# Gate's edge stage: the weighted values of a batch in two PSUM banks instead of SBUF

## The chip, the cores and the metric

The kernel runs on one core of one Trainium2 chip. The metric is the device time of one execution in microseconds; lower is better. The time given is the median of three runs. The profile is of one further execution.

## The reference

The reference is a graph network of four layers over 3125 nodes with 256 features, each a graph step and a mixture of experts. The change lies in the third layer's mixture of experts, whose gate is itself a small graph attention over 65536 edges (numbered below 4096; the nodes are 3125) with 4 heads of 4 values:

```python
h = (x_flat @ W_gat).reshape(M, HEADS, NUM_EXPERTS)      # 4 heads, 4 experts
src = jnp.concatenate([edge_index[0], loops])
dst = jnp.concatenate([edge_index[1], loops])
a_src = (h * att_src).sum(-1)
a_dst = (h * att_dst).sum(-1)
e = jax.nn.leaky_relu(a_src[src] + a_dst[dst], negative_slope=0.2)
e_max = jax.ops.segment_max(e, dst, num_segments=M)
ee = jnp.exp(e - e_max[dst])
denom = jax.ops.segment_sum(ee, dst, num_segments=M)
alpha = ee / (denom[dst] + 1e-16)
msg = h[src] * alpha[:, :, None]
agg = jax.ops.segment_sum(msg, dst, num_segments=M).reshape(M, HEADS * NUM_EXPERTS) + b_gat
```

The scores of the experts come from a layer norm of agg, and the best two of four are taken for each node.

## The kernel before

The program is a chain of phases, each a block in which the five engines (TensorE, VectorE, ScalarE, GpSimd, and SyncE for DMAs) run their own instruction lists and meet at its end. gate_graph calls gate_nodes, gate_edges and gate_scores one after the other. The change is in gate_edges alone.

gate_edges takes the 65536 edges as 512 tiles (GTILES) of 128, one edge on each partition, in 64 batches (NBG) of 8 tiles (GB). A node's row in DRAM, src_rows, has GV = 20 numbers: 16 values (W = 4 heads x 4) and 4 source logits. The destination node is split into a low part (which of 128 partitions) and a high part (which of NT = 25 groups).

The lists are written out by hand; counting semaphores are all that orders one engine behind another. For batch n:

- GpSimd (lines 2601 to 2606) issues 8 indirect DMAs, each of which gathers the 128 source rows of a tile into srow, which holds four batches. Before batch n it waits until batch n-4 has been weighed.
- ScalarE: `turned` (2682) makes hotT, the transposed one-hot of the low part, by Abs and Relu over 1024 columns; `straight` (2691) makes hot_lo, the same not transposed, by eight Abs and one Relu, into two buffers; `exps` (2700) takes the exponentials of z in place. Its order is exps(n), straight(n+1), turned(n+3).
- TensorE: `expand` (2726) multiplies hotT with the destination logits into ps_d (four PSUM tensors); `sums` (2735) adds, for each tile, hot_lo times wide (128 x 500) into ps, one PSUM bank that collects all 64 batches. Its order is expand(n+2), sums(n).
- VectorE: `logits` (2638) makes hot_hi, the one-hot of the high part (2642); picks from ps_d by it (2647), reduces (2649), forms the bound roof (2650, 2653), waits for the gathered rows and adds them (2652), and ends with z (2654, 2655). `weigh` (2657) waits for the exponentials (p_made), copies them into columns 16 to 19 of val (2660), multiplies the gathered values by them into columns 0 to 15 (2661), and makes wide, for each of the eight tiles, as hot_hi times val over 25 x 20 elements (2667). Its order is logits(n+1), weigh(n).

val and z hold two batches each, in SBUF; so does wide. A 128 x 500 product of float32 shows as two matmul records. Chain.link is an instruction followed by a wait for its end; Chain.note only counts it, and settle waits for all counted.

## Time and profile before

| | |
|---|---|
| median of 3 runs | 6740.1 us (6735.69 to 6743.65) |
| the profiled execution | 6737.76 us |
| its span, first to last instruction | 6736.0 us |
| mean granted TensorE clock | 0.889 of full |
| edge stage of the gate, first gather to copy of its result | 3687.8 to 4434.1 us |
| busy over the span: TensorE, VectorE, GpSimd, ScalarE | 5019.1, 4015.7, 2880.0, 2395.2 us |

A share of busy time over the whole span says little here, as each phase has another limit. What counts for the change is which engine waits for which within 3687 to 4434 us. In the rows, PE is TensorE's matmul, PEld its weight load, DVE VectorE, ACT ScalarE, POOL GpSimd, SPq the DMA queue of SyncE; L2667 is line 2667. A POOL row of an indirect DMA is the time that GpSimd takes to issue it, not the time until the data are there.

### The profile page before, as it was taken

What the parts mean: (1) busy time and instruction counts of PE and PEld (TensorE: products, weight loads), DVE (VectorE), ACT (ScalarE), POOL (GpSimd) and SP (SyncE); (2) the same over time, 40 slices, a digit from 0 to 9 for tenths busy, and PEclk for the clock granted to TensorE, in tenths of its full rate; (3) what the DMA queues carried; (4) which work ended last, traced back from release to release, by engine and by line L of the source; (5) the groups of instructions that cost most, each with busy time, mean ns of one, the idle gap of its engine ahead of it and who ended that gap; (6) DMA issues with size and microseconds to landing.
All of it is one profiled execution on the core that took longest, in us unless ns stands there. A gap on an engine that the chain in (4) does not pass through costs nothing. (4 is left out here: it accounts for less than half of the span.)

```text
span 6736.0 us, 84585 instructions
## 1 busy us (share of the span) xinstructions
PE 5019.1 (75%) x20905; PEld 3341.9 (50%) x21058; DVE 4015.7 (60%) x8457; ACT 2395.2 (36%) x5749; POOL 2880.0 (43%) x2895
## 2 busy tenths in 40 slices
PE   0678669368769577747774888879889995566998
PEld 0344336244437434434443444457678884455776
DVE  5577723557782477757776777741257875893112
ACT  0333212133332234423442555522225552562333
POOL 1577232357730177617761777710037764000000
PEclk9799869679988799979996899989899997896999
DMA  3444233144420144524441111100059996551000
GB/s 91 131 136 135 50 98 124 60 121 135 136 59 15 59 133 135 124 85 135 133 119 37 31 31 31 28 15 13 11 191 360 358 352 171 168 157 10 14 9 24
DMA packets 455530, 711.58 MB, mean 106 GB/s; under 512 B 105113, under 2 KB 334038, under 8 KB 455014
## 3 DMA queue, kind: packets, MB, share of 16 engines
q0 software_dynamic: 142432, 380.88, 20.7%
q1 hardware_dynamic: 310442, 318.36, 15.1%
q10 hardware_dynamic: 2304, 8.52, 0.3%
q8 instruction: 114, 1.87, 0.1%
q14 instruction: 238, 1.95, 0.1%
HBM read 604.94 MB, written 102.97 MB: 105 GB/s over the span
## 5 line engine op out<-in xcount | busy, mean ns | idle before, releaser
L666 POOL DMA_INDIRECT l_edges_stage<-l_h_rows,src_t x832 | 801.4, 963 | 329.2 <-issue 250.9
L2169 POOL DMA_INDIRECT l_edge_kv<-l_kv_rows,src_t x416 | 459.1, 1104 | 746.6 <-POOLq L2082 559.6
L2605 POOL DMA_INDIRECT l_gate_edges_srow<-l_gate_src_rows,l_gate_edges_idx x512 | 569.8, 1113 | 248.5 <-issue 155.8
L904 PE MATMUL l_edges_ps_sum<-l_edges_msg,l_edges_hot 128*128 128x264 f32 x1664 | 542.2, 449 | 173.7 <-DVE l_attn_acc L776 87.2
L2739 PE MATMUL l_gate_edges_ps<-l_gate_edges_wide,l_gate_edges_hot_lo 128*128 128x500 f32 x1024 | 502.1, 649 | 114.8 <-DVE l_gate_edges_wide L2667 114.8
L904 PEld LDWEIGHTS l_edges_ps_sum<-l_edges_msg,l_edges_hot 128*128 128x128 f32 x1664 | 280.1, 200 | 457.8 <-DVE l_attn_acc L776 321.8
L666 POOL DMA_INDIRECT l2b_edges_stage<-l2b_h_rows,src_t x416 | 401.2, 964 | 171.6 <-issue 121.8
L666 POOL DMA_INDIRECT l2a_edges_stage<-l2a_h_rows,src_t x416 | 400.2, 962 | 165.0 <-issue 121.5
L776 DVE TENSOR_TENSOR l_attn_acc<-l_attn_acc,l_edges_ps_sum 128x264 f32 x832 | 350.5, 421 | 82.0 <-DVE l_attn_acc L776 36.9
L2739 PEld LDWEIGHTS l_gate_edges_ps<-l_gate_edges_wide,l_gate_edges_hot_lo 128*128 128x128 f32 x1024 | 210.5, 211 | 366.0 <-issue 221.7
L2270 PE MATMUL l_edge_ps_e<-l_edge_w,l_edge_eaT 128*128 128x256 f32 x1664 | 376.4, 379 | 0.0
L2390 DVE SCALAR_TENSOR_TENSOR l3f_acc<-l_experts_psb,l3f_g,l3f_acc 128x256 f32<-128x256 f32 x200 | 96.8, 484 | 444.8 <-PE l_experts_psb L2421 444.8
L904 PE MATMUL l2b_edges_ps_sum<-l2b_edges_msg,l2b_edges_hot 128*128 128x272 f32 x832 | 275.9, 457 | 103.4 <-DVE l2b_edges_msg L757 55.1
L904 PE MATMUL l2a_edges_ps_sum<-l2a_edges_msg,l2a_edges_hot 128*128 128x272 f32 x832 | 271.3, 451 | 103.7 <-DVE l2a_edges_msg L757 55.2
L2270 PEld LDWEIGHTS l_edge_ps_e<-l_edge_w,l_edge_eaT 128*128 128x128 f32 x1664 | 316.5, 190 | 43.2
L2451 ACT ACTIVATE l_experts_hT<-l_experts_psa,l_experts_sc_pair 128x320 f32<-128x320 f32 x320 | 197.5, 617 | 343.5 <-PE l_experts_psa L2412 323.5
L2667 DVE TENSOR_TENSOR l_gate_edges_wide<-l_gate_edges_hot_hi,l_gate_edges_val 128x500 f32<-128x500 f32 x512 | 307.5, 673 | 6.9 <-DVE l_gate_edges_val L2660 0.5
L2696 ACT ACTIVATE l_gate_edges_hot_lo<-col,l_gate_edges_nlo 128x128 f32<-128x128 f32 x512 | 156.4, 388 | 338.4 <-PE l_gate_edges_ps L2739 338.4
L1152 PE MATMUL l_agg_ps<-l_agg_msg,l_agg_hot 128*128 128x264 f32 x832 | 210.0, 410 | 83.0 <-DVE l_attn_acc L1117 69.3
L757 DVE TENSOR_TENSOR l_edges_msg<-l_edges_stage,l_edges_ps_p 128x1056 f32<-128x1056 f32 x208 | 259.4, 1247 | 18.0 <-issue 17.1
L823 ACT ACTIVATE l_edges_hot<-col,nrel_t 128x128 f32<-128x128 f32 x832 | 263.1, 386 | 4.2 <-issue 2.7
L1561 PE MATMUL l_experts_psb<-l_experts_w,l_experts_hT 128*128 128x256 f32 x1200 | 263.6, 379 | 0.0
(773 smaller groups left out, 10745.9 us busy)
## 6 DMA issues: line engine op xcount, KB each, us to landing
l_val_rows<-l_edge_vj SPq DMA_DIRECT2D x104, 512.0 KB, 5.4
l_agg_stage<-l_val_rows SPq DMA_DIRECT2D x52, 1024.0 KB, 5.5
l_edge_ea<-in_edge_attr SPq DMA_DIRECT2D x388, 128.0 KB, 5.0
l_edges_rel_b<-rel_rows SPq DMA_DIRECT2D x52, 512.0 KB, 4.1
l_experts_w<-in_L_ffn_w SPq DMA_DIRECT2D x32, 512.0 KB, 4.7
l_gate_edges_lo_b<-l_gate_edges_lo_rows SPq DMA_DIRECT2D x64, 256.0 KB, 3.2
l_edges_stage<-l_h_rows,src_t POOLq DMA_INDIRECT x832, 2.8
l2a_edges_rel_b<-rel_rows SPq DMA_DIRECT2D x26, 512.0 KB, 4.0
```

The lines of the kernel that those rows point to most:

```text
L666: nc.gpsimd.indirect_dma_start(out=stage[:, c % SL, u, :], out_offset=None, in_=h_rows, in_offset=bass.IndirectOffsetOnAxis(ap=K.src_t[:, ...
L757: nc.vector.tensor_tensor(msg[:, g % 2, :, 0:HW].rearrange("p u (h c) -> p u h c", c=HC), stage[:, i % SL, g * GR:(g + 1) * GR, 0:HW].rear ...
L776: nc.vector.tensor_tensor(to, to, ps_sum[u][:], ALU.add).then_inc(added, 1)
L823: ins = nc.scalar.activation(hot[:, g, u, :], K.col[:], ACT.Abs, bias=K.nrel_t[:, bass.ds(t, 1)])
L904: nc.tensor.matmul(ps_sum[u][:], hot[:, g, u, :], msg[:, g % 2, u, :], start=True, stop=True).then_inc(summed, 1)
L1152: nc.tensor.matmul(ps[u][:], hot[:, n % 2, u, :], msg[:, n % 2, u, :], start=True, stop=True).then_inc(summed, 1)
L1561: last = nc.tensor.matmul(psb[(v * GT + t) % 2][:], hT[:, v % 2, f, t * P:(t + 1) * P], w2_s[:, a, f, :], start=(f == 0), stop=(f == FC - 1))
L2169: nc.gpsimd.indirect_dma_start(out=kv[:, m, u, :], out_offset=None, in_=kv_rows, in_offset=bass.IndirectOffsetOnAxis(ap=K.src_t[:, n * EB ...
L2270: last = nc.tensor.matmul(ps_e[h][:, u, :], eaT[:, n % ES, 2 * h + u, c, :], w[:, c, :], start=(c == 0), stop=(c == DC - 1))
L2605: nc.gpsimd.indirect_dma_start(out=srow[:, n % 4, u, :], out_offset=None, in_=src_rows, in_offset=bass.IndirectOffsetOnAxis(ap=idx[:, n * ...
L2667: nc.vector.tensor_tensor(wide[:, s, u], bcast(hot_hi[:, n % 3, u, :], GV), val[:, s, u, :].unsqueeze(1).to_broadcast([P, NT, GV]), ALU.mu ...
L2739: nc.tensor.matmul(flat, hot_lo[:, n % 2, u, :], wide[:, n % 2, u].rearrange("p t f -> p (t f)"), start=False, stop=False).then_inc(summed, 1)
```

## The change

val is no longer one SBUF tile for two batches but two PSUM tensors, one for each parity of n. ScalarE writes the exponentials of z straight into columns 16 to 19 of val, from where VectorE reads them as factors for columns 0 to 15. The copy of line 2660 and its settle are taken out. L2661 now reads srow (SBUF) and val (PSUM) and writes val (PSUM); L2667 reads hot_hi (SBUF) and val (PSUM) and writes wide (SBUF). There are two new waits: VectorE, before it writes z(n), waits for the exponentials of n-2 (z is read by ScalarE only now), and ScalarE, before it writes the exponentials of n, waits for the eight wide products of n-2. With ps, ps_l and four ps_d, all eight PSUM banks are taken.

```diff
-        val = ph.sb("val", [P, 2, GB, GV])
         ps = ph.psum("ps", [P, NT, GV])
         ps_l = ph.psum("ps_l", [P, GTILES // P, P])
+        val = [ph.psum(f"val{m}", [P, GB, GV]) for m in range(2)]
         ps_d = [ph.psum(f"ps_d{m}", [P, HALF, GH, NT]) for m in range(4)]
...
                     dve.wait_ge(s_in[n % 4], 16 * GB * (n // 4 + 1))
+                    if n >= 2:
+                        dve.wait_ge(p_made, n - 1)
                     ch.link(nc.vector.tensor_tensor(z[:, s], srow[:, n % 4, :, W:GV], a_d[:], ALU.add))
...
                     dve.wait_ge(p_made, n + 1)
-                    ch.note(nc.vector.tensor_copy(val[:, s, :, W:GV], z[:, s]))
-                    nc.vector.tensor_tensor(val[:, s, :, 0:W].rearrange("p u (h e) -> p u h e", h=GH),
-                                            srow[:, n % 4, :, 0:W].rearrange("p u (h e) -> p u h e", h=GH), bcast(z[:, s], GE), ALU.mult).then_inc(weighed, 1)
-                    ch.settle()
+                    nc.vector.tensor_tensor(val[s][:, :, 0:W].rearrange("p u (h e) -> p u h e", h=GH),
+                                            srow[:, n % 4, :, 0:W].rearrange("p u (h e) -> p u h e", h=GH), bcast(val[s][:, :, W:GV], GE), ALU.mult).then_inc(weighed, 1)
                     dve.wait_ge(weighed, n + 1)
                     dve.wait_ge(summed, 1 + GB * max(n - 1, 0))
                     for u in range(GB):
-                        nc.vector.tensor_tensor(wide[:, s, u], bcast(hot_hi[:, n % 3, u, :], GV), val[:, s, u, :].unsqueeze(1).to_broadcast([P, NT, GV]), ALU.mult).then_inc(wide_made, 1)
+                        nc.vector.tensor_tensor(wide[:, s, u], bcast(hot_hi[:, n % 3, u, :], GV), val[s][:, u, :].unsqueeze(1).to_broadcast([P, NT, GV]), ALU.mult).then_inc(wide_made, 1)
...
                     act.wait_ge(z_made, n + 1)
-                    nc.scalar.activation(z[:, n % 2], z[:, n % 2], ACT.Exp).then_inc(p_made, 1)
+                    if n >= 2:
+                        act.wait_ge(wide_made, GB * (n - 1))
+                    nc.scalar.activation(val[n % 2][:, :, W:GV], z[:, n % 2], ACT.Exp).then_inc(p_made, 1)
```

## Rows read from the trace of the kernel before

**Rows 1.** Page, costliest groups: busy, mean ns, idle before; gathers of the stage.
```profile
L2605 POOL DMA_INDIRECT l_gate_edges_srow<-l_gate_src_rows,l_gate_edges_idx x512 | 569.8, 1113 | 248.5 <-issue 155.8
```

**Rows 2.** Waits, 3692 to 4434 us: us in total, times, longest.
```profile
DVE l_gate_edges_z L2652 <- DMA l_gate_edges_srow<-l_gate_src_rows,l_gate_edges_idx: 174.9, 63, 2.9
POOL l_gate_edges_srow L2605 <- issue: 155.1, 509, 0.3
PE l_gate_edges_ps L2739 <- DVE l_gate_edges_wide L2667: 114.8, 56, 4.4
```

**Rows 3.** Timeline, one batch, 4002 to 4017 us: start, us, engine, line, idle before.
```profile
4002.43 0.95 POOL L2605 DMA_INDIRECT l_gate_edges_srow<-l_gate_src_rows,l_gate_edges_idx  x1 [0.30 <-issue]
...
4004.81 0.19 DVE L2652 TENSOR_TENSOR l_gate_edges_z<-l_gate_edges_srow,l_gate_edges_a_d 128x32 f32<-128x32 f32 x1 [2.80 <-DMA l_gate_edges_srow<-l_gate_src_rows,l_gate_edges_idx]
...
4005.47 0.41 DVE L2660 COPY l_gate_edges_val<-l_gate_edges_z 128x32 f32<-128x32 f32 x1
4005.56 0.32 DVE L2661 TENSOR_TENSOR l_gate_edges_val<-l_gate_edges_srow,l_gate_edges_z 128x128 f32<-128x128 f32 x1
4005.99 4.80 DVE L2667 TENSOR_TENSOR l_gate_edges_wide<-l_gate_edges_hot_hi,l_gate_edges_val 128x500 f32<-128x500 f32 x8
4006.18 1.31 POOL L2605 DMA_INDIRECT l_gate_edges_srow<-l_gate_src_rows,l_gate_edges_idx  x1 [0.30 <-issue]
...
4007.80 1.46 POOL L2605 DMA_INDIRECT l_gate_edges_srow<-l_gate_src_rows,l_gate_edges_idx  x1 [0.30 <-issue]
...
4009.56 1.47 POOL L2605 DMA_INDIRECT l_gate_edges_srow<-l_gate_src_rows,l_gate_edges_idx  x1 [0.30 <-issue]
...
4009.85 0.21 ACT L2702 ACTIVATE l_gate_edges_z<-l_gate_edges_z 128x32 f32<-128x32 f32 x1
...
4010.72 0.36 DVE L2642 TENSOR_TENSOR l_gate_edges_hot_hi<-col,l_gate_edges_hi 128x200 f32<-128x200 f32 x1
...
4011.11 1.06 DVE L2647 TENSOR_TENSOR l_gate_edges_picked<-l_gate_edges_ps_d,l_gate_edges_hot_hi 128x400 f32<-128x400 f32 x2
4011.33 0.95 POOL L2605 DMA_INDIRECT l_gate_edges_srow<-l_gate_src_rows,l_gate_edges_idx  x1 [0.30 <-issue]
...
4016.20 0.19 DVE L2652 TENSOR_TENSOR l_gate_edges_z<-l_gate_edges_srow,l_gate_edges_a_d 128x32 f32<-128x32 f32 x1 [2.79 <-DMA l_gate_edges_srow<-l_gate_src_rows,l_gate_edges_idx]
```

**Rows 4.** Timeline, edge stage of the first layer, a gather inside L757.
```profile
701.76 1.25 DVE L757 TENSOR_TENSOR l_edges_msg<-l_edges_stage,l_edges_ps_p 128x1056 f32<-128x1056 f32 x1
702.13 0.94 POOL L666 DMA_INDIRECT l_edges_stage<-l_h_rows,src_t  x1 [0.30 <-issue]
```

**Rows 5.** Timeline, edge stage of the fourth layer, a gather inside L2290.
```profile
5300.12 1.23 DVE L2290 TENSOR_TENSOR l_edge_kv<-l_edge_kv,l_edge_e_s 128x1024 f32<-128x1024 f32 x1 [1.02 <-ACT l_edge_e_s L2226]
5300.40 1.77 POOL L2169 DMA_INDIRECT l_edge_kv<-l_kv_rows,src_t  x1 [0.30 <-issue]
```

**Rows 6.** Instructions of the tile srow: duration ns min/median/max, first and last start.
```profile
L2605 POOL DMA_INDIRECT l_gate_edges_srow<-l_gate_src_rows,l_gate_edges_idx x512: 941/947/1477, 3687.8 to 4412.4; - x171
```

**Rows 7.** Groups by form: shapes, count, busy us, mean ns, idle before.
```profile
L757 DVE TENSOR_TENSOR l_edges_msg<-l_edges_stage,l_edges_ps_p 128x1056 f32<-128x1056 f32 x208 | 259.4, 1247 | 18.0 <-issue 17.1 <-ACT l_edges_ps_p L839 0.9
...
L2647 DVE TENSOR_TENSOR l_gate_edges_picked<-l_gate_edges_ps_d,l_gate_edges_hot_hi 128x400 f32<-128x400 f32 x128 | 67.5, 569 | 10.9 <-PE l_gate_edges_ps_d L2731 8.7
...
L839 ACT ACTIVATE l_edges_ps_p<-l_edges_x 128x128 f32<-128x128 f32 x52 | 14.6, 281 | 336.4 <-DVE l_edges_x L751 329.7 <-issue 6.6
...
L2667 DVE TENSOR_TENSOR l_gate_edges_wide<-l_gate_edges_hot_hi,l_gate_edges_val 128x500 f32<-128x500 f32 x512 | 307.5, 673 | 6.9 <-DVE l_gate_edges_val L2660 0.5
```

**Rows 8.** TensorE: its timeline, and windows (busy of PE, PEld, DVE, ACT, POOL, PEclk, DMA).
```profile
3995.42 8.64 PE L2739 MATMUL l_gate_edges_ps<-l_gate_edges_wide,l_gate_edges_hot_lo 128*128 128x500 f32 x16 [2.51 <-DVE l_gate_edges_wide L2667]
...
4006.82 6.95 PE L2739 MATMUL l_gate_edges_ps<-l_gate_edges_wide,l_gate_edges_hot_lo 128*128 128x500 f32 x16 [1.00 <-DVE l_gate_edges_wide L2667]
4013.60 1.92 PE L2731 MATMUL l_gate_edges_ps_d<-l_gate_edges_ad,l_gate_edges_hotT 128*128 128x100 f32 x16
...
3710.00:4410.00 700.00, 589.61 (x1964) 320.75 (x1964) 512.15 (x1173) 359.97 (x733) 550.04 (x493) 0.92 0.17 29
```

## The prediction, made before the changed kernel was run

> **What bounds the kernel now.** I read the page first: a span of 6736.0 us on one core, in the table above, and, among its costliest groups, the 512 indirect gathers of line 2605 with 569.8 us busy and 248.5 us idle [rows 1]. Those gathers belong to the edge stage that the change touches. The profiled execution's own time is 6737.76 us, 1.76 us more than its span, and 2.3 us below the median of 6740.1 us.
>
> Then the waits of that stage, 3692 to 4434 us [rows 2]. VectorE waits 63 times for the gathered rows, 174.9 us in all, and for nothing else of size. GpSimd, which issues the gathers, waits for nobody: its 155.1 us are 509 gaps of 0.3 us between one gather and the next. TensorE waits 114.8 us for VectorE's wide products. So the order is: GpSimd bounds VectorE, and VectorE bounds TensorE. The stage is as long as GpSimd's queue of gathers; every other engine has spare time in it.
>
> Then one batch in order of time [rows 3]. The reader should see three things. The batch runs from one z addition (L2652) at 4004.81 to the next at 4016.20, 11.39 us, with 2.79 us of waiting before the second. Eight gathers fill that period: those that start outside the wide products take 0.94 or 0.95 us, and the three that start at 4006.18, 4007.80 and 4009.56, while L2667 runs (4005.99 to 4010.79), take 1.31, 1.46 and 1.47 us. And the gather at 4011.33, which starts inside L2647 (4011.11 to 4012.17), takes 0.95 us. L2667 reads two tiles in SBUF (hot_hi, val); L2647 reads one in PSUM and one in SBUF.
>
> So the question is what lengthens a gather. **The same contrast in other stages.** A gather that starts at 702.13, inside the 1.25 us product L757 (operands in SBUF and PSUM), takes 0.94 us [rows 4]. A gather that starts at 5300.40, just inside L2290 (1024 elements a partition, both operands in SBUF), takes 1.77 us [rows 5]. The delay behaves as a wait until the running instruction has finished reading: the largest delay beside L2667 is 1.47 - 0.95 = 0.52 us, just under the 0.59 us from one L2667 to the next (eight in 4.80 us, the last lasting 0.67: 4.13/7), and beside L2290, 1.23 us long, it is 0.82 us for a gather that starts 0.28 us in. I take this mechanism: a VectorE instruction with both inputs in SBUF holds back a gather that starts within it, one with an input in PSUM does not.
>
> The Trainium skill, SBUF — State Buffer, section "Who interferes with whom", says the first half: a VectorE instruction with two SBUF inputs contends with a GpSimd instruction that reads SBUF, and one with at most one SBUF input does not. The trace agrees (1.47 against 0.95 us). The same section also says that tensor_tensor was not seen to stall DMA; that sentence is rival B's.
>
> **The change, part by part.**
> 1. *val moves to PSUM; L2667 and L2661 now have one operand in each memory.* By the rows above, no gather is held back by them any more. The whole excess of the gathers is 569.8 us busy [rows 1] less 512 times their median of 0.947 us [rows 6], 484.9 us: **84.9 us**. The gathers are back to back in both versions, so this comes off the end of the queue: a period of 8 x (0.947 + 0.305) = 10.0 us in place of 11.39, the gap being 155.1/509 [rows 2]. Cross-check: three slow gathers a batch, 0.36 + 0.51 + 0.52 = 1.39 us, over the 62 batches whose wide products have gathers beside them (the last two have none) is 86 us.
> 2. *The copy L2660 is gone.* It delays the next instruction by 0.09 us (4005.47 to 4005.56) [rows 3]. VectorE sits idle 2.79 us a batch, so 62 of the 64 copies give nothing; the last two, behind the last gather, give 0.2 us.
> 3. *Price of PSUM on VectorE.* Reading: L2647 takes 569 ns for 400 elements, L2667 673 for 500, L757 1247 for 1056 [rows 7]; a line through the two with PSUM gives (1247 - 569)/656 = 1.03 ns an element and 672 ns at 500, so L2667 should stay at 0.67. Writing: no row of VectorE writes to PSUM. From below, L2661 could gain up to 0.1 us; from above I allow 0.3 us, its own whole length (0.32) again [rows 3]. I take 0: the nearest row is ScalarE's write of 128 x 128 to PSUM, 281 ns [rows 7], and it is no longer than L2661. Cover: VectorE's own work is 11.39 - 2.79 = 8.60 us a batch, 8.5 without the copy, against the new 10.0. It waits about 1.5 us a batch for the gathers still, and that hides all of this. Without that cover 0.3 us would be 19 us over 64 batches.
> 4. *ScalarE writes its exponentials to PSUM.* 64 instructions of 0.21 us; the exponential of a batch runs at 4009.85 and its use comes behind the L2652 of 4016.20 [rows 3], over 6 us later. With the period 1.4 us shorter it is still over 3 us early, even if ScalarE were to lose a period's cut twice. Free.
> 5. *New waits.* VectorE, before z(n) is written, waits for exponential n-2; VectorE itself has waited for that one earlier, in the weighing of n-2. ScalarE, before exponential n, waits for the wide products of n-2; those precede z(n) in VectorE's own order, and ScalarE waits for z(n) anyway. Both are met when reached; queued behind them are the rest of the logits and ScalarE's hot_lo, and neither is held. At nothing. SP's queue and GpSimd's are moved past nothing; the gathers' own wait (buffer of four batches back) is met now, as the 0.3 us gaps show [rows 2], and stays so with VectorE one batch behind the gathers.
> 6. *What is late next.* After 10.0 us for GpSimd come TensorE and VectorE. TensorE at full clock needs 6.78 us (4006.82 to 4013.60, where the next 16 begin) plus 1.92 = 8.7 us a batch [rows 8]; the stretch of 700 us shows it busy 589.61 us at a mean granted clock of 0.92 [rows 8], 84%, which is 9.6 us a batch. That is 0.4 us under 10.0: near, but under. Batches caught by a low stretch of the clock (8.64 for 6.95 us [rows 8]) are made up later, as the products, one-hots and gathered rows are buffered two to four batches deep.
>
> **Sum.** Against the profiled execution: 6737.76 - 84.9 - 0.2 = 6652.7 us; plus the 2.3 us by which the median lies higher, **6655 us**, 1.3% faster.
>
> **Where it could fall short.** L2642 still reads two tiles in SBUF (200 elements). It starts 4010.72 - 4004.81 = 5.91 us after L2652 now, and 5.8 us in the new version. The landing that frees L2652 comes 2.38 us after the start of the batch's last gather (4002.43), so L2642 would run at 8.2 to 8.5 us on a scale on which gathers start at 7.5 and 8.75. It misses them by 0.2 us. A VectorE that is 0.2 to 0.5 us slower a batch would be hit, and would hold back one gather a batch by up to 200/500 of 0.52 = 0.2 us: 13 us over the stage.
>
> **Rivals.**
> - *A, freed gathers, but part lost*: L2642 meets a gather each batch (+13 us), or TensorE becomes the bound at 10.0 to 10.4 us (up to 0.4 x 63 = +25 us). 6668 to 6680. For it: the small margins of 0.2 and 0.4 us. Against: the batch of 8.64 us at a low clock came behind a pause of TensorE of 2.51 us [rows 8], and the pauses become shorter. Chance 0.25.
> - *B, gathers don't speed up*: what holds a gather back is something else that runs beside L2667 (its write into SBUF, say). The period stays 11.39 and only 0.2 us of the end goes: 6740 us. Against: L2647 and L757 write into SBUF too, and the gathers in them are at 0.95 and 0.94 [rows 3, 4]. Chance 0.07. The Trainium skill, in the section named, reports tensor_tensor not stalling a DMA issued from GpSimd, with the reason (marked inferred) that descriptor generation needs the port to write; by that rule the time would be this one. The 1.77 us of rows 5 speaks against it for gathers, which read an index column from SBUF.
> - *C, slower*: the wide product reads val as rows of 20 elements, repeated 25 times from PSUM, and that reading falls to one element in two cycles. It decides as soon as VectorE's batch passes 11.39 us: (11.39 - 8.5)/8 = 0.36 us more for each L2667. At twice the step of 0.59 less its fixed part of about 0.07, +0.52 us, the batch takes 8.5 + 8 x 0.52 = 12.7 us and the stage 64 x 1.3 = 83 us longer: 6823 us. Against: L757, with PSUM on the repeated operand, and L2647, with it on the plain one, both run at 1.03 ns an element [rows 7]. Chance 0.03.
> - *The forecast*, 6648 to 6662: chance 0.65.
>
> **Chances and range.** A measurement of this kernel can tell about 0.2%, 13 us, from no change (6727 to 6753). Forecast and A are faster, 0.90; B is same, 0.07; C slower, 0.03. The range takes in the forecast and A, with 5 us around for the spread of runs: 6645 to 6685.
>
> **What the profile after would show.** Right: line 2605 at 485 us busy with a mean of 0.95 us; z additions 10.0 us apart; VectorE's wait for the gathers near 1.5 us a batch, about 95 us in all; L2667 still 0.67 us though it reads PSUM; L2661 between 0.2 and 0.6. A shows gathers of 1.0 to 1.15 us beside L2642, or VectorE waiting for TensorE. B shows gathers of 1.46 us beside L2667. C shows L2667 above 1 us and no wait for gathers. The prediction is wrong if the mean gather stays above 1.05 us, or if gathers are no longer back to back.

## The result, and the profile after

The changed kernel takes **6644.6 us** (median of 4 runs, 6640.3 to 6656.01) against 6740.44 us of the kernel before (4 runs, 6735.69 to 6743.65): a ratio of 0.9861, with a 95% interval of 0.9844 to 0.9878. The forecast of 6655 us is a ratio of 0.9874 and lies inside it. The median itself lies 10 us below the forecast and 0.4 us below the lower end of its range, 6645 us; the interval, taken of 6740.1 us, spans 6635 to 6658 us. The profiled execution took 6656.01 us with a span of 6654.2 us. (Line numbers from L2652 on are two or three higher after: the z addition is L2654, the weighing L2662, the exponential L2704, the long matmuls L2741, the short ones L2733. The wide products are L2667 in both.)

The page's row of the gathers, which answers to [rows 1] (busy us, mean ns, idle before):

```profile
L2605 POOL DMA_INDIRECT l_gate_edges_srow<-l_gate_src_rows,l_gate_edges_idx x512 | 483.6, 944 | 249.4 <-issue 155.7
```

The mean fell from 1113 to 944 ns, 569.8 - 483.6 = 86.2 us in all. The view of the gathered tile's instructions answers to [rows 6] (duration min/median/max in ns, first and last start in us):

```profile
L2605 POOL DMA_INDIRECT l_gate_edges_srow<-l_gate_src_rows,l_gate_edges_idx x512: 940/944/1007, 3679.8 to 4318.2; - x171
```

No gather takes longer than 1.007 us, where it was up to 1.477. First to last start is 638.4 us in place of 724.6: the same 86.2 us. Since the gathers are back to back in both kernels, the whole of what they lost in length came off the stage.

The waits of the stage, 3690 to 4350 us, answer to [rows 2] (us in total, times, longest):

```profile
ACT l_gate_edges_hot_lo L2696 <- PE l_gate_edges_ps L2741: 255.7, 62, 8.5
POOL l_gate_edges_srow L2605 <- issue: 153.6, 504, 0.3
DVE l_gate_edges_z L2654 <- DMA l_gate_edges_srow<-l_gate_src_rows,l_gate_edges_idx: 101.6, 63, 2.7
PE l_gate_edges_ps L2741 <- DVE l_gate_edges_wide L2667: 79.0, 61, 3.0
```

The order is the one of before: GpSimd waits for nobody, VectorE waits 63 times for gathered rows, TensorE for the wide products. Only the amounts shrank. Neither of the two new waits (VectorE for an exponential, ScalarE for wide products of two batches back) has a row.

One batch in order of time, 4000.9 to 4011 us, answers to [rows 3]:

```profile
4000.95 0.26 DVE L2654 TENSOR_TENSOR l_gate_edges_z<-l_gate_edges_srow,l_gate_edges_a_d 128x32 f32<-128x32 f32 x1 [1.53 <-DMA l_gate_edges_srow<-l_gate_src_rows,l_gate_edges_idx]
...
4001.69 0.29 DVE L2662 TENSOR_TENSOR l_gate_edges_val<-l_gate_edges_srow,l_gate_edges_val 128x128 f32<-128x128 f32 x1
4002.01 4.77 DVE L2667 TENSOR_TENSOR l_gate_edges_wide<-l_gate_edges_hot_hi,l_gate_edges_val 128x500 f32<-128x500 f32 x8
4002.24 0.94 POOL L2605 DMA_INDIRECT l_gate_edges_srow<-l_gate_src_rows,l_gate_edges_idx  x1 [0.30 <-issue]
...
4003.49 0.94 POOL L2605 DMA_INDIRECT l_gate_edges_srow<-l_gate_src_rows,l_gate_edges_idx  x1 [0.30 <-issue]
...
4005.59 0.18 ACT L2704 ACTIVATE l_gate_edges_val<-l_gate_edges_z 128x32 f32<-128x32 f32 x1
...
4005.99 0.94 POOL L2605 DMA_INDIRECT l_gate_edges_srow<-l_gate_src_rows,l_gate_edges_idx  x1 [0.30 <-issue]
...
4006.70 0.36 DVE L2642 TENSOR_TENSOR l_gate_edges_hot_hi<-col,l_gate_edges_hi 128x200 f32<-128x200 f32 x1
...
4007.24 0.94 POOL L2605 DMA_INDIRECT l_gate_edges_srow<-l_gate_src_rows,l_gate_edges_idx  x1 [0.30 <-issue]
...
4010.96 0.25 DVE L2654 TENSOR_TENSOR l_gate_edges_z<-l_gate_edges_srow,l_gate_edges_a_d 128x32 f32<-128x32 f32 x1 [1.57 <-DMA l_gate_edges_srow<-l_gate_src_rows,l_gate_edges_idx]
```

The batch is 10.01 us long (11.39 before). The gathers that start inside L2667 take 0.94 us, like all others, and VectorE still waits 1.5 us for the rows.

How the stage stands to the whole: from its first gather to the gate's reciprocal it took 3679.8 to 4343.4 = 663.6 us, before 3687.8 to 4439.0 = 751.2 us, so 87.6 us less. The span fell by 81.8 us. Ahead of the stage the profiled run was 8.0 us earlier; behind it 13 us went the other way, in the fourth layer's edge stage (its gathers, L2169, took 693.2 us from first to last in place of 680.3). Those 13 us are spread between executions and not the change: in r1 below, the stretch from the gate's reciprocal to the next layer's sums takes 1750.9 us with the changed kernel, 1750.4 in the kernel before and 1763.5 in this execution. The 8.0 us ahead of the stage recur in r1, r3 and r4, which have val in PSUM (first gather at 3680.3, 3679.8 and 3675.7 us), and not in r2 (3690.2); whether they belong to the change is not shown.

### The profile page after: what moved, and what is told of

Read it like the earlier page. It is cut to its first block and busy times, and to the rows that moved or that the text cites. A ratio compares the mean times of both kernels' runs of the same rounds, so it can differ in the third digit from the quotient of the medians.

```text
span 6654.2 us, 84797 instructions
## 1 busy us (share of the span) xinstructions
PE 4985.8 (75%) x21057; PEld 3321.4 (50%) x21058; DVE 4006.3 (60%) x8393; ACT 2392.6 (36%) x5749; POOL 2796.2 (42%) x2895
## 5 line engine op out<-in xcount | busy, mean ns | idle before, releaser
L2169 POOL DMA_INDIRECT l_edge_kv<-l_kv_rows,src_t x416 | 463.9, 1115 | 751.1 <-POOLq L2082 557.3
L2605 POOL DMA_INDIRECT l_gate_edges_srow<-l_gate_src_rows,l_gate_edges_idx x512 | 483.6, 944 | 249.4 <-issue 155.7
L2741 PE MATMUL l_gate_edges_ps<-l_gate_edges_wide,l_gate_edges_hot_lo 128*128 128x500 f32 x1024 | 449.6, 593 | 79.0 <-DVE l_gate_edges_wide L2667 79.0
L2741 PEld LDWEIGHTS l_gate_edges_ps<-l_gate_edges_wide,l_gate_edges_hot_lo 128*128 128x128 f32 x1024 | 191.5, 192 | 297.3 <-issue 263.4
L2667 DVE TENSOR_TENSOR l_gate_edges_wide<-l_gate_edges_hot_hi,l_gate_edges_val 128x500 f32<-128x500 f32 x512 | 305.3, 668 | 2.2
L757 DVE TENSOR_TENSOR l_edges_msg<-l_edges_stage,l_edges_ps_p 128x1056 f32<-128x1056 f32 x208 | 259.3, 1247 | 18.0 <-issue 17.1
L904 PEld LDWEIGHTS l2b_edges_ps_sum<-l2b_edges_msg,l2b_edges_hot 128*128 128x128 f32 x832 | 139.3, 198 | 243.2 <-DVE l2b_attn_acc L776 160.0
```

The source lines that it names most:

```text
L757: nc.vector.tensor_tensor(msg[:, g % 2, :, 0:HW].rearrange("p u (h c) -> p u h c", c=HC), stage[:, i % SL, g * GR:(g + 1) * GR, 0:HW].rear ...
L904: nc.tensor.matmul(ps_sum[u][:], hot[:, g, u, :], msg[:, g % 2, u, :], start=True, stop=True).then_inc(summed, 1)
L2169: nc.gpsimd.indirect_dma_start(out=kv[:, m, u, :], out_offset=None, in_=kv_rows, in_offset=bass.IndirectOffsetOnAxis(ap=K.src_t[:, n * EB ...
L2605: nc.gpsimd.indirect_dma_start(out=srow[:, n % 4, u, :], out_offset=None, in_=src_rows, in_offset=bass.IndirectOffsetOnAxis(ap=idx[:, n * ...
L2667: nc.vector.tensor_tensor(wide[:, s, u], bcast(hot_hi[:, n % 3, u, :], GV), val[s][:, u, :].unsqueeze(1).to_broadcast([P, NT, GV]), ALU.mu ...
L2741: nc.tensor.matmul(flat, hot_lo[:, n % 2, u, :], wide[:, n % 2, u].rearrange("p t f -> p (t f)"), start=False, stop=False).then_inc(summed, 1)
```

## The experiments

"Stage" is the time from its first gather to the gate's reciprocal; "period" is the mean distance of the z additions ((last - first)/63). The kernel before has 751.2 and 11.27 us, the changed one 663.6 and 9.91. The ratios are to the kernel before on the same chip.

Three chips are behind them, and the times on them are not alike. Where r1 to r4 ran, the kernel before takes 6730.35 us (13 runs), as in the result. Where r5 to r8 ran it takes 8027.74 us (27 runs), and where r9 to r12 ran 8007.51 us (12 runs). What that does to the change is the matter of r9. Each chip was measured on one occasion, so what is said of a chip below can also belong to the occasion.

**r1: the changed kernel again, beside the next three.**

> The changed kernel again, for a narrower interval. The theory (gathers are no longer held back; 84.9 us off GpSimd's queue) expects a ratio near 6655/6740 = 0.987, gathers of 0.944 us on average and 10.0 us between z additions. If the gain above 85 us in the first comparison belonged to the change and was not the spread between executions, the ratio stays at 0.986 or below and the profile shows more than 88 us gone between the first gather and the gate's reciprocal.

Measured: 6643.7 us, ratio 0.9867 (0.9851 to 0.9884). Stage 665.6 us, period 9.92, VectorE's wait for gathers 102.3 us. The tile view's row is that of above within 2 ns. The stage is 85.6 us shorter than before, not over 88, and the medians differ by 86.7 us: what the first comparison (95.8 us between medians) had beyond 85 did not come again.

**r2: the copy goes, val stays in SBUF.** ScalarE writes its exponentials straight into val, with the two waits of the change; the wide products still read two tiles in SBUF.

```diff
-ch.note(nc.vector.tensor_copy(val[:, s, :, W:GV], z[:, s]))
 nc.vector.tensor_tensor(val[:, s, :, 0:W] ..., srow ...,
-    bcast(z[:, s], GE), ALU.mult)
+    bcast(val[:, s, :, W:GV], GE), ALU.mult)
...
-nc.scalar.activation(z[:, n % 2], z[:, n % 2], ACT.Exp)
+nc.scalar.activation(val[:, n % 2, :, W:GV], z[:, n % 2], ACT.Exp)
```

> From the kernel before: only the copy goes; val stays in SBUF and ScalarE writes the exponentials straight into it, with the two new waits of the change. L2667 still reads two SBUF tiles. The theory expects no change: 6738 to 6742 us, gathers of 1.46 us beside L2667, mean 1.11 us. The rival that the gain is VectorE's saved copy (64 times 0.4 us busy, or a shorter chain from exponential to products) expects 6715 us or less.

Measured: 6723.98 us, ratio 0.9988 (0.9979 to 0.9998); stage 744.4 us. The gain of the change is not here. But some 7 us are, where nothing was expected. The timeline of r2 shows why:

```profile
4005.74 4.80 DVE L2668 TENSOR_TENSOR l_gate_edges_wide<-l_gate_edges_hot_hi,l_gate_edges_val 128x500 f32<-128x500 f32 x8
4006.06 1.18 POOL L2605 DMA_INDIRECT l_gate_edges_srow<-l_gate_src_rows,l_gate_edges_idx  x1 [0.30 <-issue]
...
4007.54 1.47 POOL L2605 DMA_INDIRECT l_gate_edges_srow<-l_gate_src_rows,l_gate_edges_idx  x1 [0.30 <-issue]
```

The second and third gather inside the products are held as before, to 1.46 and 1.47 us. The first takes 1.18 us in place of the 1.31 of [rows 3]: without the copy the products start 0.32 us ahead of it, before 0.19, so it waits for a shorter rest of the first product. The 62 first ones are 1.185 us in the mean, 1.287 before. Over all 512 gathers the mean is 1100 for 1113 ns, 6.6 us, and the stage is 6.8 us shorter. So an instruction that VectorE had time for did cost something, through where the next one stood against the gathers.

**r3: val in PSUM, the copy stays.**

```diff
-val = ph.sb("val", [P, 2, GB, GV])
+val = [ph.psum(f"val{m}", [P, GB, GV]) for m in range(2)]
...
-ch.note(nc.vector.tensor_copy(val[:, s, :, W:GV], z[:, s]))
+ch.note(nc.vector.tensor_copy(val[s][:, :, W:GV], z[:, s]))
```

> From the kernel before: val goes to two PSUM banks, but VectorE's copy stays (z to val in PSUM) and ScalarE takes the exponentials in place in z. L2667 reads SBUF and PSUM. The theory expects the whole gain: the time of the changed kernel within 5 us (6640 to 6660), gathers of 0.95 us, since the copy sits within 1.5 us of VectorE's waiting. The rival that the copy counts expects 6715 to 6740 us here.

Measured: 6647.36 us, ratio 0.9877 (0.986 to 0.9893); stage 664.1 us, period 9.91, VectorE's wait 91.7 us (r1: 102.3). The whole gain is here: it is the place of val and nothing else. The copy takes 0.1 to 0.2 us a batch out of VectorE's wait, and the mean gather, 944 ns, is that of the changed kernel.

**r4: half and half.** Within one kernel, the wide products of tiles 0 to 3 read their weighted values from PSUM (valp) and those of tiles 4 to 7 from SBUF (val); copy and weighing are done in two halves.

```diff
-val[:, s, u, :].unsqueeze(1).to_broadcast([P, NT, GV])
+(valp[s][:, u, :] if u < HALF else val[:, s, u - HALF, :]).unsqueeze(1).to_broadcast([P, NT, GV])
```

> A dose between the two kernels: val of tiles 0 to 3 of each batch in PSUM, of tiles 4 to 7 in SBUF, so four of the eight L2667 read two SBUF tiles. The theory expects the gathers that start in the first half of the products at 0.95 us, two a batch in the second half at 1.3 to 1.46 us, a period of 10.7 to 10.9 us and 6685 to 6705 us. A rival by which anything else that runs beside the products holds the gathers back (writes into SBUF, TensorE's or ScalarE's reads) expects no difference between the halves.

Measured: 6693.3 us, ratio 0.9945 (0.9925 to 0.9965); stage 715.5 us, period 10.71. The timeline of r4 has both kinds side by side:

```profile
4011.06 2.43 DVE L2671 TENSOR_TENSOR l_gate_edges_wide<-l_gate_edges_hot_hi,l_gate_edges_valp 128x500 f32<-128x500 f32 x4
4011.11 0.94 POOL L2606 DMA_INDIRECT l_gate_edges_srow<-l_gate_src_rows,l_gate_edges_idx  x1 [0.30 <-issue]
...
4012.36 0.95 POOL L2606 DMA_INDIRECT l_gate_edges_srow<-l_gate_src_rows,l_gate_edges_idx  x1 [0.30 <-issue]
...
4013.41 2.44 DVE L2671 TENSOR_TENSOR l_gate_edges_wide<-l_gate_edges_hot_hi,l_gate_edges_val 128x500 f32<-128x500 f32 x4
4013.62 1.28 POOL L2606 DMA_INDIRECT l_gate_edges_srow<-l_gate_src_rows,l_gate_edges_idx  x1 [0.31 <-issue]
...
4015.20 1.46 POOL L2606 DMA_INDIRECT l_gate_edges_srow<-l_gate_src_rows,l_gate_edges_idx  x1 [0.30 <-issue]
```

Same operation, same output in SBUF, same length of 0.61 us an instruction; only the memory of one input differs. Two gathers start in the first four and are free, two start in the second four and are held. So it is in the whole stage: the 115 gathers that start in a product with PSUM take 953 ns at most, and of the 122 that start in one without, 61 take 1.257 us in the mean and 61, which start where two products meet, 1.455. Rival B (the write into SBUF, or something else beside L2667) falls with these rows.

**r5: one wide product for two tiles** (1000 elements, four instructions a batch, val in SBUF). It asks how long a gather is held.

```diff
-for u in range(GB):
-    nc.vector.tensor_tensor(wide[:, s, u], ...).then_inc(wide_made, 1)
+for u in range(0, GB, 2):
+    nc.vector.tensor_tensor(wide[:, s, u:u + 2], ...).then_inc(wide_made, 2)
```

> From the kernel before (val in SBUF): one L2667 makes the products of two tiles, 1000 elements in place of 500, four a batch. VectorE has four instructions less. The theory (a gather that starts within an instruction with two SBUF inputs waits until that instruction has done reading) expects the longest gather at 0.95 + 1.04 = 1.98 us in place of 1.47, about two held back a batch, some 1.9 us a batch in place of 1.4, and so the stage 20 to 35 us longer than before. The rival by which VectorE's traffic merely slows GpSimd expects gathers of at most 1.5 us and the stage as before or shorter.

Measured: 8027.73 us, ratio 0.9992 (0.996 to 1.0025), on the second chip; stage 799.0 us, period 11.95. Its tile view and a stretch of its timeline:

```profile
L2605 POOL DMA_INDIRECT l_gate_edges_srow<-l_gate_src_rows,l_gate_edges_idx x512: 940/945/1951, 4850.8 to 5622.6; - x171
```

```profile
5205.37 4.53 DVE L2667 TENSOR_TENSOR l_gate_edges_wide<-l_gate_edges_hot_hi,l_gate_edges_val 128x1000 f32<-128x1000 f32 x4 [0.20 <-issue]
5205.58 1.81 POOL L2605 DMA_INDIRECT l_gate_edges_srow<-l_gate_src_rows,l_gate_edges_idx  x1 [0.30 <-issue]
...
5207.69 1.92 POOL L2605 DMA_INDIRECT l_gate_edges_srow<-l_gate_src_rows,l_gate_edges_idx  x1 [0.30 <-issue]
...
5209.82 0.36 DVE L2642 TENSOR_TENSOR l_gate_edges_hot_hi<-col,l_gate_edges_hi 128x200 f32<-128x200 f32 x1
5209.92 1.08 POOL L2605 DMA_INDIRECT l_gate_edges_srow<-l_gate_src_rows,l_gate_edges_idx  x1 [0.30 <-issue]
```

The longest hold doubled with the instruction: 1.951 - 0.945 = 1.01 us for 1000 elements, 0.53 us for 500. A batch loses (608.4 - 483.6)/64 = 1.95 us to held gathers, as expected, against 1.3 us before (84.9/64). The expected 20 to 35 us more in time did not show: the interval allows 32 us less to 20 us more, and the stage of the kernel before has no trace on this chip. And L2642, with two inputs in SBUF and 200 elements, holds one for 0.14 us here: the collision that the forecast's part on what could fall short names.

The rule behind the holds comes out of the start times. How far a gather starts into the product, plus the time by which it is held, is the same for all: 0.54 to 0.56 us for each of the 186 gathers that start in a product of 500 elements in the kernel before, 1.06 to 1.08 us for 1000 elements here, 0.23 to 0.24 us for the 200 elements of L2642. These instructions last 0.67, 1.19 and 0.36 us. So the gather is let go 0.12 to 0.13 us before the end of the instruction in whose time it starts, and the forecast's "until the running instruction has finished reading" fits; that this point is the end of the reading is an inference.

**r6: two wide products a tile** (260 and 240 elements, val in SBUF).

```diff
 for u in range(GB):
-    nc.vector.tensor_tensor(wide[:, s, u], ...)
+    for lo_t, hi_t in ((0, 13), (13, NT)):
+        nc.vector.tensor_tensor(wide[:, s, u, lo_t:hi_t], ...)
```

> From the kernel before (val in SBUF): each tile's product is made by two instructions, of 260 and 240 elements, sixteen a batch; VectorE works some 0.6 us a batch longer. The theory expects the longest gather at 0.95 + 0.27 = 1.22 us beside L2667, about 0.5 us held back a batch in place of 1.4, a period near 10.5 us and the stage about 55 us shorter than before, with nothing moved to PSUM. A rival by which the amount of SBUF traffic counts, or VectorE's work, expects the stage as before or longer.

Measured: 8096.38 us, ratio 1.0082 (1.0053 to 1.011); stage 870.6 us, period 13.10. The tile view:

```profile
L2605 POOL DMA_INDIRECT l_gate_edges_srow<-l_gate_src_rows,l_gate_edges_idx x512: 940/953/1172, 4847.1 to 5672.4; - x171
```

The longest hold halved, 1.172 - 0.945 = 0.23 us, as expected. In all 512 gathers it is 19.7 us against 84.9 before, 0.3 us a batch (0.5 expected), because most gathers start 0.18 to 0.25 us into a piece and so wait for a short rest of it. The time didn't follow: GpSimd now waits for VectorE's weighing (176.6 us in the stage), so here something other than the gathers sets the pace. That is the first sight of what r9 is about.

**r7: the changed kernel with L2642 moved onto a gather,** by one unused reduction of 300 elements ahead of it.

```diff
+if n >= 2:
+    for _ in range(1):
+        ch.link(nc.vector.tensor_reduce(junk[:, 0:3], picked[:, 0:3], AX.X, ALU.add))
 ch.link(nc.vector.tensor_tensor(hot_hi[:, n % 3], K.col ...
```

> From the changed kernel: one extra reduce of 300 elements a batch on VectorE, waited for, ahead of hot_hi (L2642), its result unused. It costs VectorE 0.5 us, which 1.5 us of waiting cover, but moves L2642, which still reads two SBUF tiles, from 0.54 us ahead of a gather's start to about its start. The theory expects one gather a batch held back by up to 0.2 us: the stage up to 13 us longer than the changed kernel's 664 to 666 us (first gather to the gate's reciprocal), mean gather up to 0.97 us. If the price named in rival A does not exist, the stage stays at 664 to 666 us.

Measured: 8084.49 us, ratio 1.0072 (1.0039 to 1.0105); stage 861.2 us. The timeline of r7 has the collision:

```profile
5299.70 0.37 DVE L2646 TENSOR_TENSOR l_gate_edges_hot_hi<-col,l_gate_edges_hi 128x200 f32<-128x200 f32 x1
5299.75 1.14 POOL L2606 DMA_INDIRECT l_gate_edges_srow<-l_gate_src_rows,l_gate_edges_idx  x1 [0.30 <-issue]
```

+0.2 us for this gather, the size that the forecast gave it, but only for the earliest: the 60 gathers that start inside L2646 are held by 0.02 to 0.20 us, 0.1 in the mean, and all 512 together are 6.1 us longer than in the changed kernel, half of rival A's 13. What that does to the time couldn't be read here, because the gathers don't bound the stage in this run (GpSimd waits 180.2 us for VectorE).

**r8 and r11: the changed kernel with 2 us more on VectorE a batch,** two unused reductions of 800 elements, on the second and on the third chip (the diff of r7 with `range(2)` and whole tiles).

> From the changed kernel: two extra reduces of 800 elements a batch on VectorE, waited for (1.02 us each), their result unused. VectorE's own work goes from 8.45 to 10.5 us a batch, above GpSimd's 10.0. The theory (1.5 us of cover a batch, then VectorE becomes the bound) expects a period of 10.5 us, the stage 30 us longer than the changed kernel's, VectorE's wait for the gathers gone and GpSimd waiting for buffers. If the cover were larger than the profile's idle time, the stage would stay; if there were none, it would be 130 us longer.

> From the changed kernel, two extra waited-for reduces a batch on VectorE (1.02 us each), their result unused, as in the call before. On a chip like the first: VectorE's own work 10.5 us a batch, 0.5 above GpSimd's 10.0, so the stage 30 us longer than the changed kernel's 664 to 666. With cover larger than the profile's idle time it would stay, with none it would be 130 us longer.

Measured: r8 8083.59 us, ratio 1.0056 (1.0021 to 1.009), stage 870.3 us; r11 8068.07 us, ratio 1.0075 (1.0051 to 1.0099), stage 856.7 us. On the third chip the changed kernel itself has a stage of 866.8 us and 8092.41 us (r9), so 2 us more a batch on VectorE cost nothing there. Since it is not VectorE's work that bounds the stage there, the cover of 1.5 us on a chip like the first was not tested by this.

**r9: the changed kernel on the third chip.**

> The changed kernel beside the three below, on whatever chip this call gets. In the call before this one the kernel before took 8028 us in place of 6730 to 6740, with TensorE's and the other engines' instructions arriving late (waits put down to nothing but issue, and to remote), so nothing of the whole time could be compared with the first call. If this chip is like the first, the theory expects a ratio of 0.987 and a stage (first gather to the gate's reciprocal) of 664 to 666 us. If it is like the second, the late instructions bound the stage in place of the gathers, and the theory expects the gathers still at 0.95 us but little or none of the 85 us: a ratio of 0.99 to 1.005.

Measured: 8092.41 us, ratio **1.0101** (1.0068 to 1.0135). On this chip the change makes the kernel slower, by 85 us, outside of what was expected. Its gathers are as free as on the first chip, and yet (page, stage's waits of 4890 to 5757 us):

```profile
L2605 POOL DMA_INDIRECT l_gate_edges_srow<-l_gate_src_rows,l_gate_edges_idx x512 | 483.4, 944 | 434.0 <-DVE l_gate_edges_val L2662 192.5
```

```profile
DVE l_gate_edges_picked L2647 <- remote: 320.9, 32, 22.7
PEld l_gate_edges_ps L2741 <- issue: 229.7, 801, 25.3
ACT l_gate_edges_hot_lo L2696 <- remote: 212.2, 30, 7.9
POOL l_gate_edges_srow L2605 <- DVE l_gate_edges_val L2662: 192.5, 30, 8.6
```

GpSimd waits for VectorE, and VectorE, in every second batch, waits 10 us ahead of its first use of what the short matmuls of TensorE made ("remote" stands where the trace couldn't name a releaser). The stage takes 866.8 us, the period is 13.07 us, in turns of 8.3 and 17.8. TensorE's own timeline in r9, two batches, and the two instructions of VectorE and ScalarE that begin late in them:

```profile
5199.73 10.00 PE L2741 MATMUL l_gate_edges_ps<-l_gate_edges_wide,l_gate_edges_hot_lo 128*128 128x500 f32 x16 [2.58 <-ACT l_gate_edges_hot_lo L2698]
5209.57 1.92 PE L2733 MATMUL l_gate_edges_ps_d<-l_gate_edges_ad,l_gate_edges_hotT 128*128 128x100 f32 x16
5211.33 6.90 PE L2741 MATMUL l_gate_edges_ps<-l_gate_edges_wide,l_gate_edges_hot_lo 128*128 128x500 f32 x16
5218.07 1.14 PE L2733 MATMUL l_gate_edges_ps_d<-l_gate_edges_ad,l_gate_edges_hotT 128*128 128x100 f32 x9
5220.17 0.25 PE L2733 MATMUL l_gate_edges_ps_d<-l_gate_edges_ad,l_gate_edges_hotT 128*128 128x100 f32 x1 [0.96 <-issue]
5220.87 0.25 PE L2733 MATMUL l_gate_edges_ps_d<-l_gate_edges_ad,l_gate_edges_hotT 128*128 128x100 f32 x1 [0.46 <-issue]
5221.57 0.80 PE L2733 MATMUL l_gate_edges_ps_d<-l_gate_edges_ad,l_gate_edges_hotT 128*128 128x100 f32 x5 [0.46 <-issue]
5225.71 8.97 PE L2741 MATMUL l_gate_edges_ps<-l_gate_edges_wide,l_gate_edges_hot_lo 128*128 128x500 f32 x16 [3.34 <-ACT l_gate_edges_hot_lo L2698]
```

```profile
5221.69 1.06 DVE L2647 TENSOR_TENSOR l_gate_edges_picked<-l_gate_edges_ps_d,l_gate_edges_hot_hi 128x400 f32<-128x400 f32 x2 [9.46 <-remote]
5221.96 2.44 ACT L2696 ACTIVATE l_gate_edges_hot_lo<-col,l_gate_edges_nlo 128x128 f32<-128x128 f32 x8 [6.25 <-remote]
```

The short matmuls that L2647 waits for at 5221.69 are not those that run then, but those of 5209.57. (L2647 of batch n+1 comes just ahead of the weighing of n, whose products the long matmuls of 5225.71 read; and TensorE's order puts the short matmuls of n+1 ahead of the long ones of n-1.) By their rows they ended at 5211.49. The trace also keeps the time at which each semaphore rises: the one that these matmuls raise at their end rises at 5221.60, 10.1 us later, and those of the long matmuls of 5211.33, for which ScalarE waits, rise in a burst from 5221.64 on. Over the stage of r9, 33 of the 64 semaphore rises of short matmuls come more than 1 us behind their end, 30 of them by 10.1 to 11.7 us. On the first chip, before and after the change, all 64 come within 0.01 us. So what is late here is above all TensorE's signals (the rises of its semaphores), behind matmuls that the trace has as done (the trace's ends of matmuls are modelled, but the last of these starts at 5211.22).

From one start of the pair to the next it is 25.98 us, where two batches of the first chip's full pace need 2 x 8.7 = 17.4. The rest has three parts: the short matmuls of the second batch last 4.30 us in place of 1.92 (up to 6.1 in others), with 0.46 to 0.96 us between two of them in which nothing that the profile shows holds TensorE ("issue"); then a wait of 3.34 us for ScalarE's hot_lo, which could begin only with the late signals; and after such a pause the long ones take 8.97 or 10.00 us in place of 6.90. Those of 5225.71 run at a granted clock of 0.50, which is 1.2 GHz, at first and of 1.00, 2.4 GHz, later, as two of the windows of 2 us show:

```profile
5227.00:5229.00 2.00, 2.00 (x3) 0.67 (x3) 2.00 (x5) 0.89 (x2) 1.40 (x2) 0.50 0.12 23
...
5231.00:5233.00 2.00, 2.00 (x6) 0.92 (x5) 1.86 (x8) 0.00 (x0) 1.39 (x3) 1.00 0.08 5
```

(Columns: us, busy of PE, PEld, DVE, ACT, POOL with the number of instructions, then PEclk.)

Why then is the kernel before better off? It was only timed on these chips, not profiled. The nearest with a trace is r5, whose gathers are held too. Its period is 11.95 us, and its TensorE:

```profile
5194.75 6.95 PE L2739 MATMUL l_gate_edges_ps<-l_gate_edges_wide,l_gate_edges_hot_lo 128*128 128x500 f32 x16 [1.75 <-issue]
5201.53 1.92 PE L2731 MATMUL l_gate_edges_ps_d<-l_gate_edges_ad,l_gate_edges_hotT 128*128 128x100 f32 x16
5206.72 8.49 PE L2739 MATMUL l_gate_edges_ps<-l_gate_edges_wide,l_gate_edges_hot_lo 128*128 128x500 f32 x16 [3.27 <-issue]
```

Here the gathers still set the pace: GpSimd issues them without a wait but for 8.9 us, 8 x (1.188 + 0.305) = 11.94 us is the period, and VectorE waits 204.3 us for them. Nearly every batch has its pause ahead of the long matmuls. "Issue" is no lateness in these rows: the long matmuls start 0.13 us in the mean behind the product that they wait for, as in the changed kernel on the first chip (0.14); r5 raises that semaphore by two at a time, and the view then names no releaser. TensorE's signals of the short matmuls are late in r5 too, 34 of 64 by more than 1 us, but from the eleventh batch on by 3.5 us at most, which VectorE's wait for the gathers can cover. In r9 two batches run back to back, the signals of every second batch come 10 us late and more, its short matmuls have gaps (63.9 us over 50 batches), and on that wait VectorE, ScalarE and at last GpSimd.

Over 5000 to 5650 us of r9 the mean granted clock is 0.83, over 5000 to 5600 of r5 0.92; busy time of TensorE a batch is 509.15/650 x 13.07 = 10.2 against 478.16/600 x 11.95 = 9.5 us. That is 0.7 of the 1.1 us by which the periods differ, in so far as the two chips may be compared. How the steady pace of held gathers keeps the two-batch rhythm from setting in was not shown, and what makes signals late on these two chips wasn't either. It is not that more code was loaded: the page's two queues named instruction have 114 and 239 packets in r9 as in the changed kernel's profile on the first chip. The recording of the trace is a rival that no run tests; r9's trace holds 366 of the 512 semaphore rises of the long matmuls, that of the first chip all 512.

**r10: r6 again, on the third chip.**

> From the kernel before (val in SBUF), each tile's product by two instructions of 260 and 240 elements, as in the call before. On a chip like the first the theory expects the longest gather at about 1.2 us, a period near 10.5 us and the stage about 55 us shorter than the kernel before's 744 to 751 us, without PSUM. A rival by which it is the amount of SBUF traffic or VectorE's work that counts expects the stage as before or longer.

Measured: 8053.91 us, ratio 1.0059 (1.004 to 1.0078); longest gather 1.187 us, stage 834.6 us, period 12.55. Gathers held by a mean of 0.04 us (983 against 944 ns) have a place between those of before and the freed ones on this chip: 8007.5, 8053.9 and 8092.4 us in the order in which the gathers get shorter. On the second chip that order is not there: r6 took 8096.4 us, r7 and r8 with freed gathers 8084.5 and 8083.6.

**r12: six gathers of eight.** The changed kernel with the last two gathers of each batch left out; their rows are zero.

```diff
-for u in range(GB):
+for u in range(6):
     nc.gpsimd.indirect_dma_start(out=srow ...
```

> From the changed kernel: two of the eight gathers of each batch are left out (their rows stay zero). GpSimd's queue falls to 7.5 us a batch, below VectorE's 8.45 and TensorE's 8.7. The theory expects TensorE to be the next bound, at full clock: a period of 8.7 us, the stage 1.3 x 63 = 80 us shorter than the changed kernel's, VectorE waiting for TensorE or not at all, and GpSimd waiting for VectorE's weighing. If something else bounded the stage at 10.0 us beside the gathers, it would stay near 664 us.

Measured: 7876.34 us, ratio 0.983 (0.9796 to 0.9865); stage 657.0 us, 209.8 less than r9's, period 9.71. The expectation of 8.7 us, TensorE's work at full clock, was for a chip like the first; here GpSimd waits 124.3 us for VectorE, and the granted clock over 4950 to 5450 us is 0.96. The run has one surprise for r9's question: with fewer gathers, which were not what r9 waited for, the batches come in turns of mostly 8.3, 8.3 and 12.6 us in place of 8.3 and 17.8, on the same chip. So 13.07 us is not a floor that TensorE's work, the same in both, sets by itself. That the pace of the gathers and TensorE's signals act on each other is the likely reading; how, is not shown. The bound behind the gathers on a chip like the first stays unmeasured.

## Why the prediction was right, point by point

The stage gave 87.6 us in the profiled execution and 85.6 in r1, 85.1 were forecast. The rest of the 95.8 us between the first medians lies outside of what the forecast explains: it put nothing on the 8.0 us ahead of the stage, and the medians have their spread.

1. *The gathers' excess goes.* Predicted 84.9 us and a period of 10.0; measured 86.2 us between first and last gather, and 10.01 us for the batch shown. The rule behind it (held while an instruction with both inputs in SBUF reads, free with one in PSUM) is shown by r4 within one kernel, and its size by the length of the instruction: at most 0.23, 0.53 and 1.01 us for some 250, 500 and 1000 elements (r6, before, r5). The working had 0.59 us as the bound for 500; the fixed sum of start and hold puts it at 0.56.
2. *The copy gives nothing.* Right with val in PSUM: r3, with the copy, and r1, without it, can't be told apart (0.9877 and 0.9867, the intervals overlap). Wrong by itself: r2 shows some 7 us, 6.4 between the medians, that come from where the products start against the gathers. The step "VectorE has spare time, so an instruction less gives nothing" overlooked that VectorE's position, not only its length, set how long gathers were held. The sum doesn't suffer, since after the change nothing is held.
3. *PSUM costs VectorE nothing.* L2667 was put at 0.67 us and took 668 ns (673 before), L2661 at 0.32 at the most likely; its successor took 288 ns in the mean and 289 in the median. Before it was 296 in the mean but 285 in the median, and 284 in r2, which writes to SBUF without the copy ahead: so the write to PSUM costs some 4 ns, and the higher mean of before belongs to the copy. The groups by form:

```profile
L2667 DVE TENSOR_TENSOR l_gate_edges_wide<-l_gate_edges_hot_hi,l_gate_edges_val 128x500 f32<-128x500 f32 x512 | 305.3, 668 | 2.2
...
L2662 DVE TENSOR_TENSOR l_gate_edges_val<-l_gate_edges_srow,l_gate_edges_val 128x128 f32<-128x128 f32 x64 | 18.5, 288 | 0.0
...
L2704 ACT ACTIVATE l_gate_edges_val<-l_gate_edges_z 128x32 f32<-128x32 f32 x64 | 11.6, 181 | 0.0
```

   Rival C did not come true: reading a row of 20 elements 25 times over from PSUM goes at the speed of SBUF.
4. *Exponentials free.* They are made at 4005.59 and used at 4011.68, 6.1 us later (over 3 predicted), in 181 ns (0.21 us before).
5. *New waits at nothing.* No row of the waits has them.
6. *What is late next.* VectorE waits 101.6 us for gathers (about 95 predicted), 1.5 us a batch, so the gathers still bound the stage. For TensorE the forecast allowed 9.6 us a batch at the mean clock of [rows 8], 0.4 us under the period. The term that was off is that clock. TensorE over 3710 to 4310 us (busy of PE, PEld, DVE, ACT, POOL, then PEclk) has

```profile
3710.00:4310.00 600.00, 526.72 (x1934) 296.27 (x1933) 490.17 (x1080) 352.71 (x722) 453.76 (x481) 1.00 0.21 33
```

   TensorE is busy 526.72/600 of the time, 8.8 us of a period of 10.0, at a granted clock of **1.00** where it was 0.92. The long matmuls of 61 of the 64 batches take 6.89 to 6.95 us; before, those of 29 batches took 8.4 to 10.0. All of these but the first batch's came behind a pause of TensorE of 2.5 us or more, and only six batches behind such a pause ran at full clock; now the pauses are 1.3 us in the median and one batch, the last but one, has so long a one. So the mean clock of before came with the pauses, and the forecast had it as a property of the load. Rival A's half that rests on TensorE was therefore further off than it was priced.
7. *L2642.* It starts 5.75 us after the z addition (5.8 predicted) and ends at 4007.06, 0.18 us ahead of the gather at 4007.24: the predicted miss by 0.2 us, on the right side. In 4 of the 64 batches a gather does start inside it, and the longest of these takes 0.987 us. r5 and r7 show what it would have met, 0.14 us and 0.1 us a gather in the mean.

The rule of the Trainium skill, SBUF — State Buffer, section "Who interferes with whom", in its first half (two SBUF inputs contend, one doesn't) agrees with every row of r4. Its remark that tensor_tensor was not seen to stall DMA, by which rival B's 6740 us would have come out, does not hold for these gathers: they wait up to 0.53 us for a tensor_tensor of 500 elements and up to 1.01 us for one of 1000.

What the prediction did not see is that its sign hangs on the chip, or on the occasion. What it says was borne out where the kernel takes 6.7 ms. On two other chips, where it takes 8.0 ms, TensorE's signals come late, the gathers are not what the freed version waits for, and the change cost 1.0% on the one where it was timed. The prediction's condition ("gathers no longer back to back" makes it wrong) names just that, but no trace of before gave a hint of it.

## What to carry to other kernels

When a queue of gathers bounds a stage, list their durations against what VectorE runs at their start: a bimodal duration (0.94 and 1.3 to 1.5 us here) is time that an input moved to PSUM gives back in full, and where it can't be moved, instructions of half the length halve the longest hold (that this saves time was not shown: r6 and r10, on the chips of 8.0 ms, took 0.8% and 0.6% longer). Look also at where instructions stand against the gathers, since a shift of 0.13 us moved 7 us over 64 batches. And have the verdict from more than one chip: the same edit was -1.4% (-1.3% in r1) and +1.0%, and the sum of engines' busy times tells nothing of signals that come late.

## What the runs showed of the hardware that was not expected

- A gather's hold grows with the VectorE instruction that it meets: at most 0.23 us for 240 to 260 elements, 0.53 for 500, 1.01 for 1000. It ends at a fixed time after that instruction's start, 0.55, 0.29 and 1.07 us for 500, 260 and 1000 elements, wherever in it the gather starts. With one input in PSUM the gathers shown take 0.94 or 0.95 us, and the longest of all 512 takes 1.007.
- VectorE's copy is held by a gather in turn. In the kernel before it took 172 to 175 ns where it started 0.47 to 0.53 us into a gather, and 253 to 420 ns where it started 0.53 to 0.70 us into one. With PSUM as its target (r3) it took 184 to 189 ns beside the same gathers.
- PSUM as an operand cost VectorE next to nothing: its product of 500 elements took 668 ns reading it against 673 with both inputs in SBUF, its write of 128 elements 289 against 284 or 285 ns in the median. ScalarE's write of 32 elements took 181 against 213 ns.
- With shorter pauses of TensorE ahead of the long matmuls (1.3 us in place of 2.5 to 3.1 us in half of the batches) its granted clock in the stage was 1.00 in place of 0.92; with pauses of 2.6 to 3.4 us in every second batch (r9) it was 0.83.
- One and the same kernel before took 6730 to 6740 us where the result and r1 to r4 were measured, 8008 and 8028 us on two other chips. There TensorE's semaphores rise 10.1 to 11.7 us behind the end of the short matmuls that raise them, in every second batch of r9, where it is 0.01 us on the first chip, and TensorE is idle for 0.46 to 0.96 us between short matmuls of one group with no releaser. The edge stage of the first layer, which the change doesn't touch, is longer too: its gathers run from 208 to 2520 us in place of 210 to 1926. The cause was not found.
